# Recurrent stage: reciprocal root on VectorE, small work on ScalarE, and another order of the parts

## The reference

```
x = x + gnn(layernorm(x), adj)          # agg = adj^T ((x_ln @ eW) / rowsum(adj));  h_t = tanh(agg_t @ Wx + h_{t-1} @ Wh + b)
x = x + ffn(layernorm(x))               # 16 experts, top 2 of the gate's logits, softmax over the two
#   moe = sum_k w_k * (relu(x_ln @ w1[e_k] + b1[e_k]) @ w2[e_k] + b2[e_k])
#   out = layernorm(x_ln + moe) * gamma + beta
```

## Time and profile before

| | |
|---|---|
| median of 3 runs | 715.17 us (713.19 to 716.28) |
| profiled execution | 712.58 us, its span 710.7 us |
| first to last tanh | starts at 74.6 and 258.6 us |
| scatters of the recurrent stage on GpSimd | 93.7 to 286.8 us |
| first load of the experts' stage | 291.2 us |

### The profile page before, as it was taken

One profiled execution on the slowest core, in us unless ns is written; L12 is line 12 of the kernel. 1 busy time (PEld: TensorE's weight loads), 2 busy tenths in 40 slices (PEclk: granted clock), 3 DMA queues, 4 the chain that ended last, 5 costly groups with the idle time before them and its releaser, 6 DMA issues.

```text
span 710.7 us, 17699 instructions
## 1 busy us (share of the span) xinstructions
PE 545.0 (77%) x4140; PEld 486.8 (68%) x4140; DVE 523.0 (74%) x2695; ACT 376.8 (53%) x1185; POOL 500.3 (70%) x557
## 2 busy tenths in 40 slices
PE   2666897988888872399999999900799999999920
PEld 1555575765666661299999999900799999999920
DVE  5996697887877775188888888700299899999850
ACT  2999443333333320266666666500588888888810
POOL 3677568888888887167777777776067777777774
PEclk9999999898988955599999999955699999999975
DMA  8999469322323213369876665441997676664110
GB/s 244 273 283 304 127 217 258 103 81 89 92 88 94 73 49 114 76 191 324 282 244 207 198 198 179 154 152 28 302 318 223 192 219 203 197 210 143 46 51 7
DMA packets 115094, 121.37 MB, mean 171 GB/s; under 512 B 19017, under 2 KB 99613, under 8 KB 115008
## 3 DMA queue, kind: packets, MB, share of 16 engines
q1 hardware_dynamic: 95936, 76.79, 37.7%
q0 software_dynamic: 17920, 43.03, 16.7%
q10 hardware_dynamic: 1152, 0.56, 0.3%
HBM read 68.67 MB, written 55.90 MB: 175 GB/s over the span
## 4 chain that ended last, share of the span: by engine, by line
PE 38%; ACT 7%; POOL 7%; issue 4%; DMA 1%; DVE 1%; SPq 0%; POOLq 0%; ACTq 0%; DVEq 0%
PE bank L931 19%; PE bank L947 15%; ACT hs L999 5%; POOL rows_by_second L212 4%; POOL out_dram L212 3%; PE bank L920 3%; ACT xT L980 2%; PE bank L944 2%; DMA R<-rows_by_second 0%; DMA rows_by_second<-R 0%; DMA R<-rows_by_first 0%; ACT wr L988 0%; SPq L856 0%; ACT L1008 0%; SPq L858 0%
## 5 line engine op out<-in xcount | busy, mean ns | idle before, releaser
L212 POOL DMA_INDIRECT out_dram<-R x144 | 143.2, 995 | 67.5 <-issue 39.0
L212 POOL DMA_INDIRECT rows_by_second<-R x144 | 144.7, 1005 | 62.3 <-issue 35.1
L947 PE MATMUL bank<-W,hs 128*128 x1152 | 176.8, 290 | 0.0
L999 ACT ACTIVATE hs<-bank,wr 128x128 f32<-128x128 f32 x432 | 127.1, 366 | 87.6 <-PE bank L931 81.8
L931 PE MATMUL bank<-xT,wr 128*128 128x128 f32 x1152 | 158.9, 282 | 7.1 <-ACT xT L980 7.1
L947 PEld LDWEIGHTS bank<-W,hs 128*128 128x128 f32 x1152 | 152.4, 193 | 3.8 <-issue 0.2
L931 PEld LDWEIGHTS bank<-xT,wr 128*128 128x128 f32 x1152 | 143.1, 196 | 14.4 <-ACT xT L980 14.4
L212 POOL DMA_INDIRECT rows_by_first<-st x128 | 126.7, 989 | 35.7 <-issue 33.8
L1068 DVE SCALAR_TENSOR_TENSOR R<-bank,R 128x128 f32<-128x128 f32 x288 | 87.3, 344 | 66.2 <-PE bank L947 62.7
L988 ACT COPY wr<-W1b 128x258 f32 x288 | 104.9, 426 | 17.1 <-PEq L802 17.0
L537 ACT ACTIVATE HT<-bank,bcol 128x128 f32<-128x128 f32 x128 | 46.7, 364 | 95.2 <-PE bank L450 93.9
(11 more groups left out here) (132 smaller groups left out, 856.9 us busy)
## 6 DMA issues: line engine op xcount, KB each, us to landing
R<-rows_by_second SPq DMA_DIRECT2D x144, 196.0 KB
R<-rows_by_first SPq DMA_DIRECT2D x144, 68.0 KB
xq<-in_x_dram SPq DMA_DIRECT2D x32, 256.0 KB, 3.6
aq<-in_adj_dram SPq DMA_DIRECT2D x32, 256.0 KB, 4.2
x2r<-in_x_dram SPq DMA_DIRECT2D x32, 256.0 KB, 2.8
rows_by_second<-filler SPq DMA_DIRECT2D x1, 3136.0 KB, 13.2
rows_by_second<-filler SPq DMA_DIRECT2D x16, 196.0 KB
rows_by_second<-R POOLq DMA_INDIRECT x144
```

What stands on the lines that cost most here:

```text
L212: return nc.gpsimd.indirect_dma_start(dst, bass.IndirectOffsetOnAxis(ap=idx, axis=0), src, None, bounds_check=limit[n], oob_is_err=False)
L947: i = mm(o, hs[:, h, c, k * P:(k + 1) * P], W2[:, bass.ds(e[k], 1), c, :].rearrange("p o f -> p (o f)"), start=False, stop=c == 1, skip_gr ...
L999: i = a(hs[:, h, c, k * P:(k + 1) * P], ps_h[c][h][:, k * P:(k + 1) * P], ACT.Relu, bias=wr[:, u % 2, 2 * h + k, F + c:F + c + 1])
```

## The change

On GpSimd `rstd` goes, and `send` comes two quads behind instead of three. It also waits for two more semaphores (`s_tok`, `s_w1`).

On VectorE the reciprocal root is made in nine small operations of 128 x 4 elements: a start value from the bits of the number (`root_0`), and twice a step of four operations (`sq`, `ag`, `in`, `ou`), each of which waits for the one before. Their places lie among the others in `order`. `soft_1`, the copy of the tokens' numbers (L693), the product `C_NMR` (L614) and `centre_1` to `centre_3` go.

On ScalarE come the tokens' copy (`tokens`), the sum for the softmax (`sums`), and the centring of W2 in two operations for each quad (`w2_mean`, `w2_centre`). Its loop body has 8 quads instead of 4.

On TensorE the product of 512 columns becomes four of 128, one behind each step; `turn_x(q-1)` comes behind step 2, `count(q-2)` behind it, and `logits(q-1)` behind step 3.

In the experts' stage only the operands of one operation change (mean and root in place of root and product; L1046).

```diff
-C_RSTD, C_NMR, C_W1, C_W2, C_TOKEN, C_POS1, C_POS2, C_SPARE = range(P, P + 8)
+C_MEAN, C_RSTD, C_W1, C_W2, C_TOKEN, C_POS1, C_POS2, C_SPARE = range(P, P + 8)
...
-            def rstd(q, u):
-                h = u % 2
-                pool.wait_ge(s_v2, q + 1)
-                g.tensor_tensor(st[:, u, :, C_RSTD], ve2[:, h, :], mhalf[:, 0:QUAD], ALU.pow).then_inc(s_r2, 1)
-
             def send(q, u):
 
+                hold(pool, s_tok, q + 1)
+                pool.wait_ge(s_w1, q + 1)
                 hold(pool, s_d, q + 1)
...
             def turn(q, u):
-                if beyond(q, 1):
-                    rstd(q - 1, (u - 1) % SLOTS)
-                if beyond(q, 3):
-                    send(q - 3, (u - 3) % SLOTS)
+                if beyond(q, 2):
+                    send(q - 2, (u - 2) % SLOTS)
...
-            def fresh(q, u):
-
-                return mm(ps_rnn[u % 2][:, :], Ec[:, :], AX[:, bass.ds(QUAD * q, QUAD), :], start=True, stop=True,
+            def fresh(q, u, k):
+
+                return mm(ps_rnn[u % 2][:, k * P:(k + 1) * P], Ec[:, :],
+                          AX[:, bass.ds(QUAD * q + k, 1), :].rearrange("p o b -> p (o b)"), start=k == 0, stop=True,
                           skip_group_check=True)
...
-                    if k == 0 and not (isinstance(q, int) and q == NQ - 1):
-                        fresh(q + 1, u + 1)
-                    if k == 1 and beyond(q, 1):
+                    if not (isinstance(q, int) and q == NQ - 1):
+                        fresh(q + 1, u + 1, k)
+                    if k == 0 and beyond(q, 1):
                         turn_h(q - 1, u - 1)
-                    if k == 2 and beyond(q, 3):
-                        count(q - 3, u - 3)
+                    if k == 2 and beyond(q, 1):
+                        turn_x(q - 1, u - 1)
                     if k == 2 and beyond(q, 2):
-                        logits(q - 2, u - 2)
+                        count(q - 2, u - 2)
                     if k == 3 and beyond(q, 1):
-                        turn_x(q - 1, u - 1)
+                        logits(q - 1, u - 1)
...
+            def sums(q, u):
+                act.wait_ge(s_ex, q + 1)
+                a(den[:, u % 2, :], ex[:, u % 2, :], ACT.Identity, bias=unit[:, :]).then_inc(s_den, 1)
...
-                    if k == 0 and beyond(q, 2):
-                        x1T_out(q - 2, u - 2)
-                    if k == 1 and beyond(q, 3):
-                        exps(q - 3, u - 3)
+                    if k == 0:
+                        w2_mean(q)
+                    if k == 1:
+                        w2_centre(q)
+                        tokens(q, u)
+                    if k == 2 and beyond(q, 1):
+                        x1T_out(q - 1, u - 1)
+                    if k == 3 and beyond(q, 2):
+                        exps(q - 2, u - 2)
+                        sums(q - 2, u - 2)
...
+            def against(n):
+                def part(q, u):
+                    h = u % 2
+                    dve.wait_ge(s_root, 8 * q + 4 * n + 2)
+                    v.tensor_tensor(root_b[:, h, :], root_a[:, h, :], ve2[:, h, :], ALU.mult).then_inc(s_root, 1)
+                return part
...
-                order = ((tile_a, 1), (soft_1, 3), (tile_b, 1), (soft_2, 3), (place_1, 3), (tile_b2, 1), (place_2, 3),
-                         (soft_3, 3), (tile_b3, 1), (gate_1, 2), (place_3, 3), (gate_2, 2), (gate_3, 2),
-                         (centre_1, 0), (gate_4, 2), (centre_2, 0), (gate_5, 2), (centre_3, 0))
+                order = ((gate_1, 2), (gate_2, 2), (tile_a, 1), (gate_3, 2), (gate_4, 2), (gate_5, 2), (tile_b, 1),
+                         (tile_b2, 1), (tile_b3, 1), (root_0, 1), (place_1, 2), (sq_0, 1), (place_2, 2), (ag_0, 1),
+                         (in_0, 1), (soft_2, 2), (ou_0, 1), (place_3, 2), (sq_1, 1), (ag_1, 1), (soft_3, 2),
+                         (in_1, 1), (ou_1, 1))
```

More of the change, by code:

```diff
@@ L165, in build @@
         s_sct = [sem(f"s_sct{i}") for i in range(SLOTS)]
-        s_dd, s_ex, s_w1, s_hot, s_nm, s_cnt, s_pos, s_sel, s_red, s_d, s_den, s_chain = (
-            sem("s_" + k) for k in ("dd", "ex", "w1", "hot", "nm", "cnt", "pos", "sel", "red", "d", "den", "chain"))
+        s_dd, s_ex, s_w1, s_hot, s_tok, s_cnt, s_pos, s_sel, s_red, s_d, s_den, s_chain = (
+            sem("s_" + k) for k in ("dd", "ex", "w1", "hot", "tok", "cnt", "pos", "sel", "red", "d", "den", "chain"))
         padded, starts, tables = sem("padded"), sem("starts"), sem("tables")
@@ L367, in turn @@
             def turn(q, u):
-                if beyond(q, 1):
-                    rstd(q - 1, (u - 1) % SLOTS)
-                if beyond(q, 3):
-                    send(q - 3, (u - 3) % SLOTS)
+                if beyond(q, 2):
+                    send(q - 2, (u - 2) % SLOTS)
             quads(pool, turn, SLOTS)
-            rstd(NQ - 1, SLOTS - 1)
-            for k in range(3):
-                send(NQ - 3 + k, SLOTS - 3 + k)
+            for k in range(2):
+                send(NQ - 2 + k, SLOTS - 2 + k)
         @block.tensor
@@ L475, in _ @@
             turn_h(NQ - 1, UN - 1)
[L476 to L477 removed]
+            count(NQ - 2, UN - 2)
             turn_x(NQ - 1, SLOTS - 1)
             logits(NQ - 1, UN - 1)
[L480 removed]
             count(NQ - 1, UN - 1)
@@ L604, in tile_b3, with root_0, square, part @@
                     dve.wait_ge(s_r2, q - 1)
-                v.tensor_scalar(ve2[:, u % 2, :], mvs[:, u % 2, :, 1], LN_EPS, None, ALU.add).then_inc(s_v2, 1)
+                v.tensor_scalar(ve2[:, u % 2, :], st[:, u, :, C_RSTD], LN_EPS, None, ALU.add).then_inc(s_v2, 1)
+            def root_0(q, u):
+                dve.wait_ge(s_v2, q + 1)
+                v.tensor_scalar(root_y[:, u % 2, :].bitcast(I32), ve2[:, u % 2, :].bitcast(I32), -0.5, ROOT_BITS,
+                                ALU.mult, ALU.add).then_inc(s_root, 1)
+            def square(n):
+                def part(q, u):
+                    h = u % 2
+                    dve.wait_ge(s_root, 8 * q + 4 * n + 1)
+                    v.tensor_tensor(root_a[:, h, :], root_y[:, h, :], root_y[:, h, :], ALU.mult).then_inc(s_root, 1)
+                return part
+            def against(n):
+                def part(q, u):
+                    h = u % 2
+                    dve.wait_ge(s_root, 8 * q + 4 * n + 2)
+                    v.tensor_tensor(root_b[:, h, :], root_a[:, h, :], ve2[:, h, :], ALU.mult).then_inc(s_root, 1)
+                return part
+            def inner(n, scale):
+                def part(q, u):
+                    h = u % 2
+                    dve.wait_ge(s_root, 8 * q + 4 * n + 3)
+                    v.scalar_tensor_tensor(out=root_a[:, h, :], in0=root_b[:, h, :], scalar=-10 / 3 * scale ** 2,
+                                           in1=root_b[:, h, :], op0=ALU.add, op1=ALU.mult).then_inc(s_root, 1)
+                return part
+            def outer(n, scale):
+                def part(q, u):
+                    h = u % 2
+                    dve.wait_ge(s_root, 8 * q + 4 * n + 4)
+                    y = root_y[:, h, :]
+                    i = v.scalar_tensor_tensor(out=st[:, u, :, C_RSTD] if n else y, in0=root_a[:, h, :],
+                                               scalar=5 * scale ** 4, in1=y, op0=ALU.add, op1=ALU.mult)
+                    i.then_inc(s_r2 if n else s_root, 1)
+                return part
+            sq_0, ag_0, in_0, ou_0 = square(0), against(0), inner(0, ROOT_0), outer(0, ROOT_0)
+            sq_1, ag_1, in_1, ou_1 = square(1), against(1), inner(1, ROOT_1), outer(1, ROOT_1)
             def gate_1(q, u):
@@ L755, in _ @@
             quads(dve, turn, SLOTS)
-            for q in range(NQ, NQ + 3):
+            for q in range(NQ, NQ + 2):
                 turn(q, q % SLOTS)
```

85 lines of the change are left out of this document (45 added, 40 removed).

## The result

The changed kernel takes 736.71 us (median of 4 runs, 732.31 to 736.77), the kernel before 714.82 us (4 runs, 713.19 to 716.28): a ratio of 1.0286, with a 95% interval of 1.0254 to 1.0318. It is slower by 21.9 us. Forecast were 722.0 us, and 707 to 735. The sign was right, and so was the new bound, VectorE; the size was three times too small, and the time lies outside the range. One of the first four runs was at 732.3 too, and three at 736.7: 4 us of the 21.9 are such a difference between runs of the same kernel.

A forecast was written before the change was run, and what follows sets the result against it. GpSimd bounds before, VectorE after: first `tile_a` 82.0, first turn 4.5, thirty turns of 6.09, jumps 6.8, clock 3, giving 279.0; last scatter 293.6, 6.8 later, so 715.2 + 6.8 = 722.0 us; range 707 to 735.

The forecast's parts named there:

- The bound: Recurrent stage: VectorE takes GpSimd's place as bound, 6.09 us a quad against GpSimd's 5.11.
- The sum: Recurrent stage: `tile_a(31)` at 279.0 us, last scatter ending at 293.6 against 286.84 before, 6.8 us later.
- The turn: VectorE's work for one quad: grows from 4.86 to 6.09 us, taken as certain to 0.2.
- The jumps back: VectorE's loop: two stalls of 3.0 us and about 0.3 at each of three bodies, no longer hidden, 6.8 us.
- The clock: TensorE falling to 1.2 GHz part of the time: 3 us over the stage, bounds 0 and 17.
- the slack: TensorE and ScalarE chain from `hot` to `turn_h`: done 0.7 us before `tile_a` needs it, at the full clock.
- the second rival: TensorE at 1.2 GHz becomes the bound in many quads: up to 14 us more, 730 to 736 us; chance 0.2.
- The first `tile_a`: Start of VectorE's first turn in the recurrent stage: at 81.97 us as before, since it waits for TensorE.
- The end: After `tile_a(31)`: VectorE's last work to 288.5 us, then GpSimd's four scatters, 5.1 us, to 293.6.
- The edits priced at nothing: ScalarE's small work covered by idle time, four input pieces hidden on TensorE, GpSimd's two added waits at nothing.
- The faster rivals: VectorE's waits cost less or are filled: full case 684 us, chance 0.13; half way 707 us, chance 0.08.
- The first rival: Waits between VectorE's small operations cost less or are filled, GpSimd bounds at 5.11 us a quad: 684 us; chance 0.13.

The follow-up runs named there:

- k3_one_step: The changed kernel with one step of the root instead of two, four dependent operations fewer (root too inexact for use): 708.4 us, ratio 0.9902 to the kernel before.
- k4_four_more: The changed kernel with four more dependent root operations on scratch copies in each VectorE turn: 754.42 us, ratio 1.0549 to the kernel before.
- k9_side_by_side: Changed kernel with the old lags and TensorE order, small work on ScalarE, nine root operations side by side at the end of VectorE's turn: 731.32 us, 1.0241.
- k16_changed: The changed kernel itself, measured again in a later set: 732.32 us beside 714.31 for the kernel before, ratio 1.0244.
- k15_filler_no_jumps: The changed kernel with two idle TensorE products ahead of each counting from the third quad on, and VectorE's turns written out without a loop: 717.99 us, 1.0045.
- k14_filler_third_chip: The changed kernel with two idle TensorE products of 512 columns ahead of each counting from the third quad on, VectorE's loop kept: 726.91 us, 1.0175.
- k7_no_jumps: The changed kernel with VectorE's 32 turns of the recurrent stage written out, no loop: 724.48 us, ratio 1.0132 to the kernel before.
- k10_small_only: The kernel before, root on GpSimd and old lags, with only the small work moved to ScalarE and the input product in four pieces: 714.8 us, 0.9997.
- k1_root_gpsimd: The changed kernel with the reciprocal root back on GpSimd, all else as changed: 727.21 us, ratio 1.0173 to the kernel before.
- k8_spread: Changed kernel with the old lags and TensorE order, small work on ScalarE, nine root operations spread over two VectorE turns, others between: 697.81 us, 0.9765.

## Why the prediction came out as it did

**The bound.** Right. VectorE took GpSimd's place; GpSimd stood idle 1.4 us or more ahead of nearly each quad's first scatter (forecast about 1). `k3_one_step` and `k4_four_more` move the time by 0.14 to 0.23 us for each root operation, and `k9_side_by_side` shows that it is the waits and not the work.

**The sum.** Forecast were 279.0 us for `tile_a(31)` and 293.6 for the end of the last scatter; the trace has 294.15 and 310.36. From the first `tile_a` to the last it is 197.0 us by the forecast, 210.9 in the profile after and 206.65 in that of `k16_changed`. Two kernels part this. `k15_filler_no_jumps`, which has neither jumps nor waits for the transposes, takes 191.5 where the forecast's terms say 4.5 + 182.7 = 187.2; `k14_filler_third_chip`, with the jumps, 201.1. So:

- **The turn** was 6.09 us by the forecast; it is 6.17, 6.23 in the loop, and in `k15_filler_no_jumps` 6.4 to 6.5 in six turns of the 31, for which the runs show no cause. In all 191.5 - 187.2 = 4.3 us too little. The step of 0.27 us behind `ou_1` accounts for 0.07 a turn, or 2.1, the first turn (4.83) for 0.3 and the six long turns for most of the rest.
- **The jumps back** were 6.8 us; they cost 201.1 - 191.5 = 9.6, of which one wait for the transposes is 1.2, and `k7_no_jumps` says 7.7. Too little by 1 to 2 us.
- **The clock** was 3 us with bounds of 0 and 17; it costs 10.5 us of waits in the profile after and 5.6 in `k16_changed`. In the profile after this is the step that failed by most. The path was right and the term was mis-sized, 3 us for about 10. It rested on two sentences: "TensorE is as idle as before in a quad of 6.1 us, so I expect the same clock", and "most is lost in the slack". The clock went from 0.87 to 0.80. Each wait is about 1 us, less than the 1.9 that I had worked out for a quad at 1.2 GHz, and there are ten of them in 30 quads: it was the number of late quads that I set too low, since I let the slack of 0.7 us absorb most of them and expected the clock of before. It was the second rival, with 0.2, that came nearest. Why the two sets differ in it, 10 waits against 6, stays open. In `k16_changed` the clock is only some 2.5 us above its term, the turn's 4.3 is the largest error, and the time of that set, 732.3, would have lain within the range: that the first set fell outside it by 1.7 us is in part chance.
- **The first `tile_a`** is at 83.24 us and not at 82.0. The first tanh starts at 76.65 us, 2.0 later than before; in all kernels that have the rest of the change it is 1.1 us or more later, and the runs don't show why. The first turn was 5.9 us in the profile after (with a wait of 0.99 for the transposes) and 4.82 in `k16_changed`, for 4.5.
- **The end.** From the last `tile_a` to the last scatter 16.2 us for 14.6. I let GpSimd wait for `place_3` of the last quad; by the rows above the scatters of the last quad but one, begun at 300.45, still ran then, and eight at 1.28 us end at 310.4.

For the profile after these are 4.3 + 2.8 (jumps and what lies with them) + 7 + 1.3 + 1.6 = 17 us, of the 17.3 between 736.7 and the forecast 719.4. The clock's 7 is 210.9 - 201.1 = 9.8, less the 3 of the forecast.

**The edits priced at nothing.** The small work on ScalarE and the input in four pieces are at nothing: `k10_small_only`, within 0.2% of before. The order was not: I costed the smaller lags at nothing, apart from the chain through `hot`. `k1_root_gpsimd` shows 12.4 us for them when GpSimd has the root. The fall of the clock belongs to them too. In `k9_side_by_side` VectorE's turn is even longer (6.3 us), but with the old lags it never waits for the transposes, and its windows view in 84 to 250 us has a clock of 0.89; in the same stretch it is 0.94 in `k8_spread` and 0.81 in `k16_changed`.

```profile
84.00:250.00 166.00, 127.27 (x930) 111.54 (x928) 142.53 (x987) 74.76 (x274) 89.68 (x92) 0.89 0.37 112
```

That no rival said "the order alone makes it slower" was a gap in the list.

**The faster rivals.** The waits do cost what the earlier trace rows say, 0.20 us. The first rival's number was nonetheless the right one for a kernel that hides them: 688.9 us, with GpSimd as the bound.

## What to carry to other kernels

A chain of tiny dependent operations costs its waits and not its work: 0.20 us each as neighbours, about 0.07 with another operation between. So where such a chain is put on a busy engine, spread it over two turns of the pipeline, with other work between any two of its steps. A shorter lag is not free even where no engine has more work: the new lags and order cost 12.4 us with the root left on GpSimd, most likely because a lag is a store of work for the engine behind. And when the bound moves, all that it used to hide must be priced again: here the jumps back (7.7 to 8.9 us) and TensorE's low clock (5.4 to 6.5), which together were more than all the rest (3.7).

## What the runs showed of the hardware

A stall at VectorE's jump back was 2.9 to 3.1 us in the order of the change, 3.2 and 3.5 in `k9_side_by_side`, and 3.8 to 3.95 in `k8_spread`, whose body has the same parts; why it is longer is not shown. Two products of 512 columns in each quad, put where TensorE waited, raised its granted clock from 0.81 to 0.96 and shortened the kernel by 5.4 us, though they were more work for the engine: TensorE's busy time in 84 to 290 us fell from 172 to 161 us.
